# Graph stage of a four-layer kernel: indirect scatters issued two at a time, each two after the last two have landed

## What is computed

```
x = x + L0_gnn(layernorm(x), adj)      # masked attention with 8 heads and an MLP
x = x + L0_ffn(layernorm(x))           # slice attention over 64 slices
x = x + L1_gnn(layernorm(x), adj)      # two graph convolutions with elu
x = x + L1_ffn(layernorm(x))           # a shared MLP and the best 2 of 8 experts for each token
```

```
out = x @ w_root + b
agg = einsum('bij,bid->bjd', mask, x) / deg ;  out = out + agg @ w_rel
h = elu(conv1(x));  h = elu(conv2(h))
```

## Time and profile before

| | |
|---|---|
| three runs | 3038.88, 3046.15, 3048.08 us; median 3046.15 |
| profiled execution, span | 3015.8 us |
| median less span | 30.35 us |
| busy in the span | PE 92%, PEld 74%, DVE 66%, ACT 48%, POOL 48% |
| graph phase | about 1686 to 2332 us of the span |
| indirect DMAs there (L1285) | 256, mean 993 ns on POOL |

### The profile page before, as it was taken

How to read it: one execution, slowest core, us unless ns; L and a number is a source line. 1 busy time by engine, 2 the same in 40 slices (tenths; PEclk the granted TensorE clock), 3 DMA queues, 4 the chain that set the end, 5 groups by cost and what they waited for, 6 DMA issues and landing times. The chain is left out here.

```text
span 3015.8 us, 88050 instructions
## 1 busy us (share of the span) xinstructions
PE 2783.1 (92%) x29020; PEld 2230.8 (74%) x29021; DVE 1983.0 (66%) x6888; ACT 1455.8 (48%) x2928; POOL 1453.6 (48%) x2403
## 2 busy tenths in 40 slices
PE   8999999899799999999998987888858999999999
PEld 4666666799677777777777666666647888888888
DVE  5666666577788888888886666666643444444453
ACT  3444444555456566566565443333433444444444
POOL 4555554333244444444444355555540455555564
PEclk8999999999899999999999999888879999999999
DMA  1111111000000000000000111111410222222265
GB/s 48 35 31 31 35 35 31 1 0 0 1 0 0 0 0 0 0 0 0 0 0 1 47 45 50 43 43 45 141 59 8 67 76 71 70 76 73 63 194 143
DMA packets 158090, 118.01 MB, mean 39 GB/s; under 512 B 20150, under 2 KB 145593, under 8 KB 158010
## 3 DMA queue, kind: packets, MB, share of 16 engines
q1 hardware_dynamic: 140602, 81.02, 9.7%
q0 software_dynamic: 17408, 35.95, 3.6%
HBM read 68.36 MB, written 48.56 MB: 39 GB/s over the span
## 5 line engine op out<-in xcount | busy, mean ns | idle before, releaser
L1977 ACT ACTIVATE e_hidden<-e_ps,e_b1g 128x512 f32<-128x512 f32 x288 | 192.0, 687 | 280.9 <-PE e_ps L90 190.7
L1934 POOL DMA_INDIRECT token_y<-e_y,e_rows x288 | 285.1, 990 | 77.9 <-issue 68.4
L815 POOL TENSOR_TENSOR s_sw<-s_expo,s_rsum 128x512 f32<-128x512 f32 x128 | 133.6, 1043 | 367.7 <-DVE s_rsum L1078 367.7
L1285 POOL DMA_INDIRECT sorted_z<-r_z,r_rows x256 | 254.2, 993 | 83.3 <-issue 83.3
L2029 PE MATMUL e_ps<-expert_w,e_hidden 128*128 x2304 | 284.9, 276 | 8.5 <-issue 8.5
L2029 PEld LDWEIGHTS e_ps<-expert_w,e_hidden 128*128 128x128 f32 x2304 | 276.3, 192 | 16.8 <-issue 10.7
L456 DVE TENSOR_REDUCE a_V<-a_ps_s 128x8 f32<-128x1024 f32 x128 | 156.9, 1226 | 179.2 <-PE a_ps_s L395 179.2
L320 ACT ACTIVATE a_probT<-a_ps_st 128x1024 f32<-128x1024 f32 x128 | 131.2, 1025 | 204.4 <-PE a_ps_st L403 204.4
L395 PEld LDWEIGHTS a_ps_s<-a_nT 16*128 16x128 f32 x2048 | 137.1, 189 | 92.0 <-issue 56.1
L2106 DVE TENSOR_TENSOR e_biased<-e_ps,expert_b 128x512 f32<-128x512 f32 x72 | 49.8, 691 | 224.7 <-remote 120.9
L395 PE MATMUL a_ps_s<-a_nT 16*128 16x128 f32 x2048 | 186.7, 301 | 11.1
(11 more groups left out here) (401 smaller groups left out, 8335.1 us busy)
## 6 DMA issues: line engine op xcount, KB each, us to landing
e_z<-sorted_z SPq DMA_DIRECT2D x72, 260.0 KB
c_y<-token_y SPq DMA_DIRECT2D x22, 512.0 KB, 4.2
X<-in_x_dram SPq DMA_DIRECT2D x32, 256.0 KB, 2.8
a_adj<-in_adj_dram SPq DMA_DIRECT2D x32, 256.0 KB, 2.8
g_adj<-in_adj_dram SPq DMA_DIRECT2D x32, 256.0 KB
out_dram<-X SPq DMA_DIRECT2D x32, 256.0 KB, 2.6
c_y_s<-token_y SPq DMA_DIRECT2D x10, 512.0 KB, 5.0
token_y<-e_y,e_rows POOLq DMA_INDIRECT x288
```

The source lines that it names most:

```text
L815: nc.gpsimd.tensor_tensor(sw[p][:, :, :], expo[p][:, :, :], rsum[p][:, 1, :].unsqueeze(2).to_broadcast([T, HEADS, C]), ALU.mult).then_inc( ...
L1285: nc.gpsimd.indirect_dma_start(sh.sorted_z, bass.IndirectOffsetOnAxis(ap=rows[own][:, e * GB + piece:e * GB + piece + 1], axis=0), zr[own] ...
L1934: nc.gpsimd.indirect_dma_start(sh.token_y, bass.IndirectOffsetOnAxis(ap=rows[p][:, b:b + 1], axis=0), y[p][:, b, :], None).then_inc(y_scat ...
L1977: nc.scalar.activation(hidden[p][:, c, :], ps_1[c % 2][:, :], ACT.Gelu, bias=b1g[p][:, c:c + 1]).then_inc(s["hidden_done"], 1)
```

## The change

POOL's step is rewritten. A function `pause` waits until the pieces of the group that have been issued have landed, and ends in a tiny addition to one more column of `g_spare`. Every `scatter` (two DMAs) now has such a wait ahead of it: pieces 1, 2 and 3 a `pause`, and piece 0 a further wait, in the addition that was there, for the whole of the group before. Piece 1 moves from step t-3 to step t-2, right behind piece 0, and piece 2 moves behind `rstd`. So `rstd` now stands behind pieces 0 and 1 of a group and ahead of pieces 2 and 3. The experts' phase and all other engines' programs are as they were.

```diff
-        carrier, spare = sb("g_carrier", [T, 3]), sb("g_spare", [T, 2])
+        carrier, spare = sb("g_carrier", [T, 3]), sb("g_spare", [T, 8])
...
+            def pause(paused, column, nth, again, own, landed):
+
+                if again:
+                    pool.wait_ge(s[paused], nth - 2)
+                pool.wait_ge(scattered[own], landed)
+                nc.gpsimd.tensor_tensor(spare[:, column:column + 1], ones[:, :], ones[:, :], ALU.add)\
+                  .then_inc(s[paused], 1)
+
             def step(t, r, k, known):
-                if live(known, 3, groups):
-                    scatter((k + 1) % 4, 1)
-                    scatter((k + 1) % 4, 2)
+                whole = 2 * GB * 16
                 if live(known, 1, groups):
...
                 if live(known, 3, groups):
-                    scatter((k + 1) % 4, 3)
+                    own, uses = (k + 1) % 4, r + (k - 3) // 4
+                    pause("third_paused", 6 + k % 2, t - 2, since(known, 5), own, uses * whole + whole // 2)
+                    scatter(own, 2)
+                    pause("last_paused", 2 + k % 2, t - 2, since(known, 5), own, uses * whole + whole * 3 // 4)
+                    scatter(own, 3)
                 if live(known, 2, groups):
+                    own, uses = (k + 2) % 4, r + (k - 2) // 4
                     if since(known, 4):
                         pool.wait_ge(s["spare_done"], t - 3)
                     pool.wait_ge(s["rows_done"], t - 1)
                     pool.wait_ge(s["gates_set"], t - 1)
                     pool.wait_ge(s["twin_done"], t - 1)
+                    if since(known, 3):
+                        pool.wait_ge(scattered[(k + 1) % 4], (r + (k - 3) // 4 + 1) * whole)
                     nc.gpsimd.tensor_tensor(spare[:, k % 2:k % 2 + 1], ones[:, :], ones[:, :], ALU.add)\
                       .then_inc(s["spare_done"], 1)
-                    scatter((k + 2) % 4, 0)
+                    scatter(own, 0)
+                    pause("second_paused", 4 + k % 2, t - 1, since(known, 4), own, uses * whole + whole // 4)
+                    scatter(own, 1)
             run_rounds(pool, step, groups, LAG, PEEL)
```

More of the change, by code:

```diff
@@ L1191, in graph_phase @@
                  "exp2_done elu2_done x_done numbered before_set setup zr_done zr_turned zrT_done "
-                 "logits_done copied spare_done best_done which_done whichf_done chosen_done either_done "
+                 "logits_done copied spare_done second_paused third_paused last_paused best_done which_done whichf_done chosen_done either_done "
                  "ranked place_done carried placed_done rowsf_done rows_done gap_done odds_done odds_step ids_set "
```

## The result

The changed kernel takes 3053.92 us (median of 7 runs, 3049.52 to 3066.74), the kernel before, on the same chip, 3038.88 (7 runs, 3033.86 to 3048.08). The ratio is 1.0053, 95% interval [1.0034, 1.0072]: 15 us between the medians, 16 by the ratio, and more than the 0.3% that can be told from no change. The forecast was 3049 us, 3 us more than the median of the kernel before then at hand (3046).

A forecast was written before the change was run, and what follows sets the result against it. Late PE signals during scatters were taken to hold the kernel, then POOL's chain (17.4 us a round). Rounds -3, long rounds +7, gaps +4, phase's end -6: together +2 to +4 us, predicted 3049 us, own range 3037 to 3062.

The forecast's parts named there:

- The late signals: Graph phase: PE's completion signals arrive late while many scatters are under way; expected to go, 17.5 to 14.7 us a round.
- At most two under way: POOL's scatters in the graph phase: with at most two under way, PE's late signals were expected to go.
- the round of 14.7: Graph-phase round without late signals: 17.5 - 2.8 = 14.7 us, expected to hide behind POOL's chain.
- POOL as the bound: Graph phase: all four pairs in one chain on POOL, each waiting for the pair ahead; POOL's round is everybody's round.
- POOL's round, 17.4 us: POOL's graph-phase chain: 1.42 + 0.1 + 0.5 + 9.24 + 4.2 + 1.92 = 17.4 us, as long as the present round.
- three landings by 1.40 with 0.1 for the release: POOL's round: open landings of the second, fourth and first pair, 1.40 us each, 4.2 us, plus release 0.1 us each.
- The mean way of 0.54: POOL, from the addition behind a landing to the first DMA: 0.34 to 0.66 us, mean 0.54 over the phase.
- -3 for the rounds, +7 and +4: Graph phase: 29 rounds by 17.4 - 17.5, -3 us; long rounds not all hidden, +7; gaps no longer covered, +4.
- the seven long rounds: Some seven of 29 rounds last about 20 us; with PE's slower clock, about 1 us over POOL's round each: +7 us.
- The phase's end, -6: End of the graph phase: ACT's wait of 2.80 us and about 3.0 of its 4.23 go, -6 us.
- The 30.35 us: Time around the profiled span up to the median, taken to stay unchanged: 30.35 us.
- The slower rival: POOL's third, fourth and first pair: landing with release 1.8 us, round 18.7, +33, 3079 us; decides from 17.8; chance 0.2.

The follow-up runs named there:

- the rolling window: Changed kernel's order, but each graph-stage scatter waits, through its own tiny addition, for the landing of the scatter before the last; 0.9903 of the kernel before.
- the order alone: Changed kernel with all waits for landings and the three added additions taken out, only the new order of pieces left; 1.0118 of the kernel before.

## Why the prediction was right or wrong

- **The late signals.** That they go is right, and shown by taking the waits out and putting them back: "remote" 79, 0, 173 us. Missed was that their price hangs on the order: I costed the moved pieces only as terms of POOL's chain. Two parts of the reading did not hold. "At most two under way" is no change: the kernel before kept to it for all but 0.5% of the time. And many signals come while the row still goes on, not when it is through. Nor did any kernel without most of the late signals reach the round of 14.7: the best were at 16.4 to 16.5.
- **POOL as the bound.** Right: `mean` waits for `rstd` in every round, and a change of POOL's chain alone moves the round (0.59 us by the place of a wait, 1.1 by one landing less) and the ratio by more than its interval (1.0053, 1.0016, 0.9912).
- **POOL's round, 17.4 us.** This term was too small: 18.35. The step was "three landings by 1.40 with 0.1 for the release", 4.5 us. Measured are 154.3 / 31 = 5.0 us a round. Most landings cost what was assumed, 1.46 to 1.52 in the round shown; seven with an adjacency load near them cost 2.0 to 2.7, together 7 us over the typical ones, where 0.06 for each landing had made 5.6. What was missed is mostly the one round beside the large transfers: 15.2 us in all, 10.7 over the 4.5. I had not looked at what SP issues at the stage's end. Two smaller terms add: a scatter takes 1.02 us instead of 0.99, 0.2 us over eight, and from `rstd` to the third pair's DMA it is mostly 0.67 us, 0.89 in the round shown (1977.37 to 1978.26), where 0.5 was put. The mean way of 0.54 held (0.55).
- **-3 for the rounds, +7 and +4.** Together +8; measured +24.7 (532.0 - 507.3). Nothing shows the seven long rounds or PE's slower clock in them as a term of its own; 11.9 us are the one round of 29.8, and 1.83 us one gap in a pair.
- **The phase's end, -6.** Measured -8.5; ACT's waits of 2.80 and 4.23 are 0.67 and 0.21.
- **The sum.** +16.2 by the traces and +15 between the medians, where +3 stood. The range 3037 to 3062 was drawn about a base of 3046, so it runs from -9 to +16, and the change lies at its upper end. That the time, 3053.92, is only 5 us off the forecast is luck: the base on this chip was 3038.88, 7 us below the median of the three runs that were at hand. The 30.35 us did no harm to the difference, but are no work around the span.
- **The slower rival** comes nearest by its place and its bound ("from 17.8 us on"), not by its price: with its release a landing isn't 1.8 us everywhere, but 1.5 mostly and up to 5 beside other transfers.
- The Trainium skill ("DMA: Bandwidth & Descriptors", section "Rules for kernel authors") says to wait late. These runs agree: the rolling window waits late and is 1.0% faster than before, where the open landings are 0.5% slower.

## What to carry to other kernels

Where many indirect scatters leave in a row, look for waits on PE that end by "remote" while the row runs. A tiny addition with its wait ahead of every scatter took most of them away here; let it wait for the scatter before the last, not for the last, so that no landing stands open. It costs POOL some 0.27 us a scatter (1.60 us from start to start on average, 1.33 in the order alone). A limit explains an effect only if it ever holds something back: count how often it did before you believe it, and take the limit out in one run. Before a new wait is priced, list every transfer that another queue issues beside it, since an open landing pays for those it meets, and check that the engine that waits keeps slack (the experts' phase had 7.2 us for what took 7.6).

## What the runs showed of the hardware

- Completions of PE reach ACT and DVE late, with waits of up to 5.8 us, while rows of scatters (128 rows of 520 bytes each) run. In the graph stage these waits sum to 173 us for rows of eight (158 with an addition between every two), 79 and 72 for rows of six, 11 and 7 for rows of four, 6 to 28 in four kernels with an addition and its waits ahead of every scatter, and 0 in the four with a landing awaited behind every pair. Which signals of PE fall into a row seems to count too: the experts' phase has 191 us with rows of four.
- Such a scatter's last packet ends 1.90 us (median) after its start on POOL, with 1.26 to 1.35 us from start to start in rows; so it was two at a time in the kernel before as well, and the late signals there can't be put down to more than two under way.
- The landing of a pair, from the record's end to the addition that waits for it: mostly 1.40 us with the wait on the addition, 1.46 to 1.52 ahead of it; 2.0 to 2.7 in 7 of 22 landings with one load of 256 KB near them, up to 5.1 beside transfers of 2 MB.
- A DMA behind an addition starts 0.34 us after it where the wait is the addition's own, 0.67 where it stands on an instruction ahead.
